# Low-rank weights and modulation columns stay in setup; the modulation rows are made beside projection and attention's opening

## What is computed

```python
x = L0_attn_x
mod = (_silu(L0_c) @ L0_wmod).reshape(L0_c.shape[0], 6, 1, -1)      # 4 x 6 x 256
sa, ca, ga, sb, cb, gb = (mod[:, i] for i in range(6))
ga = (2 * (ga >= 0) - 1) * jnp.maximum(jnp.abs(ga), 0.25)
gb = (2 * (gb >= 0) - 1) * jnp.maximum(jnp.abs(gb), 0.25)
h = _layernorm(x, axis=-1) * (1 + ca) + sa
x = x + ga * attention(h, W + B @ A / 8, ..., bo, rezero)
h = _layernorm(x, axis=-1) * (1 + cb) + sb
x = x + gb * mixture(h)
mod = (_silu(L1_c) @ L1_wmod).reshape(L1_c.shape[0], 6, 1, -1)      # the same again for block 1
```

## Time and profile before

| | us |
|---|---|
| median of three runs (lowest, highest) | 5099.54 (5083.22, 5102.6) |
| the profiled execution | 5088.73 |
| its span, first to last instruction | 5087.2 |
| setup, to the first instruction of project | 60.03 |
| project, to the first of attend | 201.5 |
| attend's opening, to its first exponential's products | 71.8 |

### The profile page before, as it was taken

One profiled execution on the slowest core, in us unless ns is written; L12 is line 12 of the kernel. 1 busy time (PEld: TensorE's weight loads), 2 busy tenths in 40 slices (PEclk: granted clock), 3 DMA queues, 4 the chain that ended last, 5 costly groups with the idle time before them and its releaser, 6 DMA issues. The chain is left out here.

```text
span 5087.2 us, 109400 instructions
## 1 busy us (share of the span) xinstructions
PE 4686.5 (92%) x35413; PEld 2578.5 (51%) x35413; DVE 4257.3 (84%) x6858; ACT 3489.3 (69%) x6724; POOL 1383.5 (27%) x1285
## 2 busy tenths in 40 slices
PE   5869999999999999999999879999699999956998
PEld 4723333333333333333333367777466666655887
DVE  5769999999999999999999868887677877875554
ACT  2438888888888888888888722322477777844554
POOL 1121111111111111111111133333334344445776
PEclk8959999999999999999999989999799999956999
DMA  4962222122222222222222111111000000044452
GB/s 157 345 146 43 52 44 49 39 47 52 44 47 42 46 52 43 44 44 45 55 44 44 33 51 41 37 50 37 22 25 24 28 20 23 25 162 148 164 164 94
DMA packets 236446, 340.01 MB, mean 67 GB/s; under 512 B 60199, under 2 KB 169762, under 8 KB 227340
## 3 DMA queue, kind: packets, MB, share of 16 engines
q1 hardware_dynamic: 219760, 275.26, 22.3%
q0 software_dynamic: 16192, 58.43, 3.1%
HBM read 205.49 MB, written 136.18 MB: 67 GB/s over the span
## 5 line engine op out<-in xcount | busy, mean ns | idle before, releaser
L816 DVE TENSOR_REDUCE at_mxp<-at_ps_m 128x2 f32<-128x1024 f32 x2092 | 2524.5, 1221 | 72.9 <-PE at_ps_m L869 53.0
L747 ACT ACTIVATE at_prob<-at_ps_s 128x512 f32<-128x512 f32 x4100 | 2228.2, 596 | 326.8 <-PE at_ps_s L859 261.7
L879 PE MATMUL at_ps_o<-at_prob,at_vs 128*32 128x256 f32 x16384 | 1313.9, 392 | 14.1 <-ACT at_osum L753 14.1
L859 PE MATMUL at_ps_s<-at_qs,at_ks 51*128 51x512 f32 x4100 | 1036.5, 500 | 5.2 <-ACT at_prob L747 5.2
L869 PE MATMUL at_ps_m<-at_ks,at_qs 49*128 49x512 f32 x4184 | 856.3, 405 | 46.5 <-DMA at_ks<-t_alibi 35.7
L859 PEld LDWEIGHTS at_ps_s<-at_qs,at_ks 51*128 51x128 f32 x4100 | 384.9, 183 | 856.6 <-ACT at_prob L747 856.1
L879 PEld LDWEIGHTS at_ps_o<-at_prob,at_vs 128*32 128x32 f32 x16384 | 323.1, 108 | 775.3 <-issue 388.5
L574 POOL TENSOR_TENSOR at_total<-at_total,at_minus 128x16 f32<-128x16 f32 x65 | 190.4, 2929 | 1118.1 <-DMA at_total<-at_osum 1118.1
L869 PEld LDWEIGHTS at_ps_m<-at_ks,at_qs 49*128 49x128 f32 x4184 | 404.0, 190 | 67.9 <-DMA at_ks<-t_alibi 36.1
L68 DVE TENSOR_TENSOR ex_hidc<-ex_hid,ex_hidc 128x512 fp32r<-128x512 f32 x128 | 158.0, 1245 | 168.9 <-ACT ex_hid L2561 168.9
L1321 PE MATMUL mi_ps_f<-mi_w,mi_act 128*128 128x256 f32 x1024 | 252.6, 391 | 15.7 <-DVE mi_acc L1179 15.7
(11 more groups left out here) (317 smaller groups left out, 6443.5 us busy)
## 6 DMA issues: line engine op xcount, KB each, us to landing
t_parts<-pr_parts SPq DMA_DIRECT2D x64, 512.0 KB, 7.1
at_ks<-t_parts SPq DMA_DIRECT2D x102, 256.0 KB
t_buf<-at_blank POOLq DMA_DIRECT2D x64, 384.5 KB, 3.2
at_qs<-t_parts SPq DMA_DIRECT2D x96, 256.0 KB
at_vs<-t_v SPq DMA_DIRECT2D x17, 1024.0 KB, 5.0
ex_rest<-t_buf SPq DMA_DIRECT2D x16, 1026.0 KB, 5.3
t_v<-pr_vaug SPq DMA_DIRECT2D x64, 256.0 KB, 5.5
first_w<-in_fw SPq DMA_DIRECT2D x16, 1024.0 KB, 7.6
```

Source lines behind the costliest of these rows:

```text
L747: nc.scalar.activation(prob[0 if up is None else (t + 1) % 2][:, j, :], ps_s[bank][:, :], ACT.Exp).then_inc(s_read, 1)
L816: nc.vector.tensor_reduce(out[:, s4, k + i, 2 * pair:2 * pair + 2], ps_m[i][:, :, :], AX.X, ALU.max).then_inc(mx_read, 1)
L859: nc.tensor.matmul(ps_s[bank][:, :], ks[s][a:a + QROWS, j // 2, t1 * P:(t1 + 1) * P], qs[s][a:a + QROWS, j // 2, c * T:(c + 1) * T], start ...
L879: last = nc.tensor.matmul(ps_o[32 * j:32 * j + 32, q0:q1], vs[s][:, t, 32 * j:32 * j + 32], prob[t % 2][:, j, q0:q1], start=(t == 0 and ha ...
```

## The change

Setup keeps the low-rank products, their additions and the modulation columns `mfm`. It no longer loads block 1's `wmod`, `bo` and `rezero`, and makes no rows. Each weight has a semaphore of its own, the small loads stand behind the first weight, and project's first two x chunks and the identity are loaded last. Block 1's `wmod` is loaded in project; PE makes both blocks' rows there ahead of its loop, and ACT copies them out of PSUM into `ro_gvec`. The ten vectors are worked out on POOL in attend's opening, between its presets, and SP stores them in the middle of its list of loads and waits for that store. The buffers are parts of tiles that the later phases fill. The core of the diff:

```diff
+def keep_rows(t, a, n):
+
+    return t[:, :, :, :].rearrange("p r b f -> p (r b f)")[:, 0:a * n].rearrange("p (a n) -> p a n", a=a)
+
+
+def rows_of(t, first, n):
+
+    return t[0:B, :, :, :].rearrange("p r b f -> p (r b f)")[:, first:first + n]
...
-        silu_c = sb("silu_c", [P, KD, 2, B])
-        wmod = sb("wmod", [P, 2, KD, 6 * D])
+        silu_c = keep["silu_c"]
+        wmod = [keep_rows(keep[name], KD, 6 * D) for name in ("sc_gvec", "mi_gvec")]
...
+                    sp.dma_start(lora_a[:, n, :], x["A" + w]).then_inc(lora_in[n], 16)
+                    sp.dma_start(lora_b[:, n, :], x["B" + w + "T"]).then_inc(lora_in[n], 16)
+                    sp.dma_start(wT[:, n, :, :], x["W" + w + "T"].rearrange("(k p) n -> p k n", p=P)).then_inc(lora_in[n], 16)
+                    if n == 0:
+                        for l in range(2):
+                            sp.dma_start(cT[:, :, l, :], x[f"c{l}T"].rearrange("(k p) b -> p k b", p=P)).then_inc(c_in, 16)
+                        sp.dma_start(bqk[:, :], x["bqk"]).then_inc(small_in, 16)
+                        sp.dma_start(keep["qscale"][:, :], x["qscale"]).then_inc(small_in, 16)
+                sp.dma_start(wmod[0], x["wmod0"].rearrange("(k p) n -> p k n", p=P)).then_inc(wmod_in, 16)
+                for h in range(2):
+                    sp.dma_start(keep[f"pr_xin{h}"][:, :, :], x["x"][h * T:(h + 1) * T, :].rearrange("(s p) f -> p s f", p=P)).then_inc(later_in, 16)
+                sp.dma_start(keep["ident"][:, :], x["ident"]).then_inc(later_in, 16)
+                sp.wait_ge(later_in, 48)
...
-                pe.wait_ge(loaded, NLOAD)
-
                 for n in range(4):
+                    pe.wait_ge(lora_in[n], 48)
                     for k in range(KD):
                         last = nc.tensor.matmul(ps[n][:, k * D:(k + 1) * D], lora_a[:, n, k * P:(k + 1) * P],
                                                 lora_b[:, n, :], start=True, stop=True)
-                last.then_inc(lora_done, 1)
+                    last.then_inc(lora_done, 1)
                 pe.wait_ge(silu_done, 1)
-
-                for j in range(3):
-                    for k in range(KD):
-                        nc.tensor.matmul(ps[4 + j][0:B, :], silu_c[:, k, 0, :], wmod[:, 0, k, j * 512:(j + 1) * 512],
-                                         start=(k == 0), stop=(k == KD - 1))
-
+                pe.wait_ge(wmod_in, 16)
                 for w, part in enumerate((1, 0, 4, 3)):
                     for k2 in range(KD):
                         for k in range(KD):
                             col = part * D + k2 * P
-                            last = nc.tensor.matmul(ps[7][:, (w * KD + k2) * B:(w * KD + k2 + 1) * B],
-                                                    wmod[:, 0, k, col:col + P], silu_c[:, k, 0, :],
+                            last = nc.tensor.matmul(ps[4][:, (w * KD + k2) * B:(w * KD + k2 + 1) * B],
+                                                    wmod[0][:, k, col:col + P], silu_c[:, k, 0, :],
                                                     start=(k == 0), stop=(k == KD - 1))
-                last.then_inc(mod0_done, 1)
-                pe.wait_ge(lora_read, 1)
-                for j in range(3):
-                    for k in range(KD):
-                        last = nc.tensor.matmul(ps[j][0:B, :], silu_c[:, k, 1, :], wmod[:, 1, k, j * 512:(j + 1) * 512],
-                                                start=(k == 0), stop=(k == KD - 1))
-                last.then_inc(mod1_done, 1)
+                last.then_inc(mod_done, 1)
 
...
+        xin = [keep[f"pr_xin{h}"] for h in range(2)]
+        wmod = [keep_rows(keep[name], KD, 6 * D) for name in ("sc_gvec", "mi_gvec")]
+        modr = [rows_of(keep["ro_gvec"], l * 6 * D, 6 * D) for l in range(2)]
...
+                sp.dma_start(wmod[1], x["wmod1"].rearrange("(k p) n -> p k n", p=P)).then_inc(wmod_in, 16)
...
-                for n in range(2):
                     rsqrt(n)
...
-                    dve.wait_ge(x_in[h], 16 * m + 16)
+                    if m is not None:
+                        dve.wait_ge(x_in[h], 16 * m)
...
+                def modulation_rows(l):
+                    for j, bank in enumerate((ps_qk[0], ps_qk[1], ps_qk[2]) if l == 0 else (ps_qk[3], ps_v[0], ps_v[1])):
+                        act.wait_ge(mod_done, 3 * l + j + 1)
+                        flat = bank[0:B, :, :].rearrange("b s f -> b (s f)") if l and j else bank[0:B, :]
+                        nc.scalar.copy(modr[l][:, j * T:(j + 1) * T], flat).then_inc(mod_read, 1)
 
                 modulate(0, 0)
+                for l in range(2):
+                    modulation_rows(l)
...
+                def modulation_rows(l):
+                    for j, bank in enumerate((ps_qk[0], ps_qk[1], ps_qk[2]) if l == 0 else (ps_qk[3], ps_v[0], ps_v[1])):
+                        flat = bank[0:B, :, :].rearrange("b s f -> b (s f)") if l and j else bank[0:B, :]
+                        for k in range(KD):
+                            last = nc.tensor.matmul(flat, keep["silu_c"][:, k, l, :], wmod[l][:, k, j * T:(j + 1) * T], start=(k == 0), stop=(k == KD - 1))
+                        last.then_inc(mod_done, 1)
+
+                modulation_rows(0)
                 transposes(0, 0)
+                pe.wait_ge(wmod_in, 16)
+                modulation_rows(1)
                 pe.wait_ge(w_cut, 2)
+                pe.wait_ge(mod_read, 6)
...
+                def modulation_rows():
+                    for l in range(2):
+                        nc.gpsimd.tensor_scalar(sgn[:, 2 * l:2 * l + 2, :], gates[l], 0.0, 2.0, ALU.is_ge, ALU.mult)
+                    pool.drain()
+                    nc.gpsimd.tensor_scalar(sgn, sgn, -1.0, None, ALU.add)
+                    pool.drain()
+                    for l in range(2):
+                        nc.gpsimd.tensor_tensor(mag[:, 2 * l:2 * l + 2, :], sgn[:, 2 * l:2 * l + 2, :], gates[l], ALU.mult)
+                    pool.drain()
+                    nc.gpsimd.tensor_scalar(mag, mag, 0.25, None, ALU.max)
+                    pool.drain()
+                    GA0, GB0, GA1, GB1 = range(4)
+                    nc.gpsimd.tensor_tensor(sgn, sgn, mag, ALU.mult)
+                    nc.gpsimd.tensor_scalar(tmp[:, 0, :], modr[0][:, 1, :], 1.0, None, ALU.add)
+                    for r, m, add in ((R_CA1, 1, 1.0), (R_SA1, 0, 0.0), (R_CB1, 4, 1.0), (R_SB1, 3, 0.0)):
+                        nc.gpsimd.tensor_scalar(rows[:, r, :], modr[1][:, m, :], add, None, ALU.add)
+                    pool.wait_ge(small_in, 32)
+                    pool.drain()
+                    for r, n in ((R_GB0, GB0), (R_GA1, GA1), (R_GB1, GB1)):
+                        nc.gpsimd.tensor_copy(rows[:, r, :], sgn[:, n, :])
+                    nc.gpsimd.tensor_tensor(rows[:, R_GCA, :], tmp[:, 0, :], sgn[:, GA0, :], ALU.mult)
+                    nc.gpsimd.tensor_scalar(rows[:, R_GRZ, :], sgn[:, GA0, :], rz, None, ALU.mult)
+                    nc.gpsimd.tensor_tensor(rows[:, R_GSA, :], modr[0][:, 0, :], sgn[:, GA0, :], ALU.mult)
+                    pool.drain()
+                    nc.gpsimd.tensor_tensor(tmp[:, 1, :], rows[:, R_GRZ, :], bo, ALU.mult)
+                    pool.drain()
+                    nc.gpsimd.tensor_tensor(rows[:, R_GSA, :], rows[:, R_GSA, :], tmp[:, 1, :], ALU.add).then_inc(rows_done, 1)
 
...
                 nc.gpsimd.memset(ks[0][96:P, :, :].bitcast(F32), 1.0).then_inc(high_set, 1)
                 pool.drain()
+                modulation_rows()
                 nc.gpsimd.memset(qs[1][:, :, :].bitcast(F32), 1.0)
+                pool.wait_ge(rows_stored, 16)
                 nc.gpsimd.memset(ks[1][:, :, :].bitcast(F32), 1.0).then_inc(ones_set[1], 1)
...
                 load_values(0, 0)
+                sp.dma_start(bo, x["bo"].partition_broadcast(B)).then_inc(small_in, 16)
+                sp.dma_start(rz, x["rezero"].partition_broadcast(B)).then_inc(small_in, 16)
...
+                sp.wait_ge(rows_done, 1)
+                sp.dma_start(d["rows"].rearrange("r b f -> b r f"), rows).then_inc(rows_stored, 16)
+                sp.wait_ge(rows_stored, 16)
                 load_vectors(sp, keep["mi_gvec"], d["rows"][R_GCA:R_GB0 + 1, :, :], later_in, later_in)
...
-        hold(until_project, wqk=([P, KD, G, P], F32), wv=([P, KD, D], F32), bqk=([P, G], F32), qscale=([P, 1], F32))
+        hold(until_project, wqk=([P, KD, G, P], F32), wv=([P, KD, D], F32), bqk=([P, G], F32), qscale=([P, 1], F32),
+             silu_c=([P, KD, 2, B], F32), pr_xin0=([P, SUB, D], F32), pr_xin1=([P, SUB, D], F32))
```

94 lines of the change are left out of this document (22 added, 72 removed).

## The result

The changed kernel took 5063.3 us, the median of 5 runs (5049.83 to 5068.34); the kernel before took 5099.54 (5083.22 to 5105.65, 5 runs beside them). The ratio is 0.9936, with a 95% interval of 0.9916 to 0.9957. The profiled execution took 5051.0 us with a span of 5049.5, against 5088.7 and 5087.2 before: 37.7 us less.

A forecast was written before the change was run, and what follows sets the result against it. Setup was taken as bound by latency and project's later part by DMA. Gains of 36.4 in setup and 4 at project's start, less 3 in attend's opening, sum to 37 us, giving 5060 us (5038 to 5080).

The forecast's parts named there:

- Setup: Setup: loads, column products and hand-over let project start at 23.6 instead of 60.03, 36.4 us gained (32 to 38.5).
- Project's start: Project's opening: first store at +21.0 against 25.2, 4 us gained; bounds a loss of 2.6 and a gain of 6.
- The named chain: Project's opening: block 1's wmod, second rows, loop products, ACT's last row copy, eviction and issue put first store at +21.6.
- The crowded start: Setup and project: low clock through both row sets, wmod1 sharing DMA with x; gain 25 to 29 us, 8 in 100.
- Attend's opening: Attend's opening: late POOL and SP's wait for the ten vectors' store lose 3 us (0 to 10).
- the term for one-input operations: POOL in attend's opening: one-input operations over 5376 elements per partition take 4.6 to 12.5 us.
- The step on the empty queue: SP in attend's opening: broadcasts start 9.9 us later, but an initially empty queue shortens the issues; 3 us lost for both chains.
- The store's landing behind w1: Attend's opening: the ten vectors' store queues behind w1's 1 MB, landing at 300.2 to 302.8, taken as 301.5.
- The serial store: Attend's opening: SP's list keeps its length, maxima come back 10 us late; gain 30 us, about 5068, 12 in 100.
- first-turn rival: Attention's first turn: warm PE gains up to 16 us (12 in 100); slower turns give 5085 to 5125 (3 in 100).
- the prediction's own sign of being wrong: Wrong if project's stretch changes over 8 us, POOL ends the opening, or attention's first turn takes another length.
- That setup would be held by x: Setup: crawling x loads hold its end and the change gives nothing, needing 37 us more loading; 3 in 100.

The follow-up runs named there:

- e5: Changed kernel with six filler products on TensorE between setup's low-rank products and column products; 5048.8 us in one run.
- e6: Changed kernel with the first chunk's transposes ahead of the first layer's rows on TensorE in project's opening; 5066.05 us in one run.
- e1: Changed kernel with the first two x chunks loaded by GpSimd at project's start again; 5073.91 us in one run.
- e4: Changed kernel with bo and rezero loaded ahead of the first keys in attend's opening; 5069.4 us in one run.
- e9: Kernel before the change with 27 one-column memsets and a drain more on GpSimd in attention's opening; 5095.14 us, ratio 1.0008 to the kernel before.
- e10: Changed kernel with 27 one-column memsets and a drain more on GpSimd in attention's opening; 5054.44 us, ratio 0.9931 to the kernel before.
- e3: Changed kernel with the first store of maxima ahead of the route phase's loads on SP; 5050.24 us in one run.
- e7: Changed kernel with twelve filler products on TensorE ahead of the wait for the maxima in attention's opening; 5115.81 us in one run.

## Why the prediction held

**The total.** 5060 was forecast and 5063.3 measured; 37 us of gain were summed, and 36.1 stand at the first exponentials' products, 37.7 in the profiled pair. The agreement within 1 us is closer than the parts deserve: between profiles, setup's end alone varies by 2 us and the opening by as much.

**Setup (36.4 forecast, 35.0 measured).** The wait for wmod ended at 16.69 instead of 15.5, and the column products took 6.96 us where I took 6.0 between 4.1 and 7.9; mfm and the hand-over took 1.4 instead of 2.1. The reason for the longer products was right: e5 brought them to 4.55 with work ahead of them. A wmod that comes 1.2 us late is the larger part of the miss, and its arrival alone varies by 2.1 us between profiles. The forecast of 23.6 for project's start lies inside the 23.05 to 25.1 that the profiles span.

**Project's start (4 forecast, 4.8 at the first store, 5.0 at its end).** I had transposes at +7.0 and the store at +21.0 by way of the second rows; they were at +7.9 and +20.3. The first rows cost 7.9 us and not 6.9, since six of the 12 products and part of the seventh went at the lower pace (before, four), but the second ran wholly at the higher one (1.88 and 3.60 us instead of 6.9), and so did the loop's first products (1.65 instead of 2.92). The named chain was right: the first products were released by ACT's last copy, and e6 shows that it binds and the transposes don't. That project's later stretch keeps its length is right too: from the issue of the first store to that of the last it took 169.8 us before and 169.2 after, so the first store 4.8 us earlier made project 5.0 shorter. (The prediction's 174 us run to the landing of one of the last stores.) The crowded start was a real danger that the early x avoided (e1).

**Attend's opening (-3 forecast, -3.9 measured).** Each step came, with other sizes. POOL's operations took 23 us, above my 12 to 20: the term for one-input operations, which I took at 4.6 to 12.5, measured 15.5, since those with arithmetic cost more than two-input ones, while the two-input term of 7.2 measured 7.7. The vectors were ready 35.1 us after attend's start and I had 34.0 (295.5 less 261.55). SP stood 5.9 us, not 3; the broadcasts were 8.4 late, not 9.9; POOL was 0.7 late at its later work, not 1.9, and that by its own 23 us: it did not stand for the store, since one preset filled that time. The step on the empty queue was right in kind: of the 8.4 us, 5.7 remained at the maxima's store and 3.0 at PE. The store's landing behind w1 was right, and e4 shows it: by the store's own way alone, 2.6 us in setup, it would have been in by 257 there, even if its long issue (2.69 us from 251.82) is added, and the broadcasts started at 258.63.

The Trainium skill (DMA: Bandwidth & Descriptors, section Queues, rings and completion order), on completions that land only behind earlier writes, agrees with e4: rows ready 3.6 us earlier, the same landing. The traces don't tell whether the store's data or only its completion came behind w1. The Trainium skill (GPSIMD Engine Reference, section 4.1, Engine selection), on one-input work at roughly line rate, does not agree with the trace for operations with arithmetic: 2.78 us for 1024 elements with one operation, against 2.34 for a two-input one of that width.

**Rivals.** The serial store was wrong in that SP's list didn't keep its length, and half right, since PE did come to wait for SP, for 3 us. Neither first-turn rival came in the profiled pair: 58.6 us against 56.3. That is luck as much as judgment, since the turn took 46 to 62 us over all profiles: the prediction's own sign of being wrong, another length of the first turn, could have come up without the change having anything to do with it. That setup would be held by x did not happen; the identity's issue took 3.85 us, but nothing waited for it.

**Not foreseen.** Route became 14 us longer. It goes with the instructions that stand ahead of it on GpSimd (e9, e10), and the mechanism is open. The profiled pair hides it behind stages that came out shorter (scan 8.1 us, expert 12.1; over all profiles scan varies by 30 us and expert by 19), so the total came out right partly by luck: such effects lie below what whole times resolve.

## What to carry to other kernels

Where a phase is a chain of latencies with idle engines, work that later phases need should leave it, and it pays in full only if its new place has slack on every queue that it passes: here 24.7 us were gained, 3.0 and 4.6 given back, the last mostly by a store placed behind a 1 MB load and ahead of a list of loads in one queue. Before work is put in ahead of a wait to bring the clock up, as in e5, look at when the wait ends: work that runs past it takes back what it gave. Load first what the next phase waits for, before its neighbour's bulk takes the DMA engines (8.6 us in e1), and put the store that an engine will wait for ahead of loads that nobody waits for yet (3 us in e3). After a change of instruction count, compare stages that it doesn't touch before explaining a few microseconds by the change itself.

## What the runs showed of the hardware that I had not expected

- GpSimd's prices by kind, from the timeline of its opening: a one-operation tensor-scalar of 4x1024 took 2.78 us (2.7 ns an element), a two-operation one of 4x512 1.91 us (3.7 ns), a two-input one of 4x1024 2.34 us (2.3 ns), a copy of 4x256 0.36 us (1.4 ns), and a memset of 128x4096 3.50 us (0.85 ns).
- Early in the execution the granted clock reads 1.00 (2.4 GHz) while the records have the lower pace. TensorE's weight loads for the row products, one for each, stand 0.85 us apart up to 30.2 and 0.43 apart from 30.7 on, and the clock of the window (last but two in its row) is the same all through. The pace, not the clock column, is what to read there:

```profile
28.00:30.00 2.00, 2.00 (x3) 0.26 (x2) 1.51 (x6) 0.00 (x0) 0.45 (x1) 1.00 0.68 219
30.18 0.13 PEld L444 LDWEIGHTS pr_psqk<-sc_gvec,silu_c 128*4 128x4 f32 x1 [0.72 <-issue]
30.70 0.09 PEld L444 LDWEIGHTS pr_psqk<-sc_gvec,silu_c 128*4 128x4 f32 x1 [0.39 <-issue]
```

- 28 idle instructions on GpSimd moved a stage 4 ms later by 11 to 12 us, up in one kernel and down in the other, each seen in two profiles.
- SP, waiting for the landing of a 40 KB store, went on 0.1 to 0.4 us after the 1 MB load ahead of it in its queue had landed, in all ten profiles with this store, whether it was issued 3 us or 7 us after that load.
- In one execution PE stood three times for 2.3 to 2.5 us without a wait that the profile shows, and each time the granted clock went from 1.00 to 0.50 (e7).
